# Passages between two graph layers placed three loop steps earlier, with two pairs of their steps put into one step each

## The reference, cut to what matters

```python
# layer 0
A = a * adj, with 1 - a added to the diagonal
y = (A / rowsum(A)) @ x
x1 = layernorm(x + relu(y @ W.T + b))
# layer 1
t = logmap0(x1)                      # a factor for each row: needs the row's norm, a log, some divisions
par = adj   * sigmoid(t @ w_par[:d] [:, None] + t @ w_par[d:] [None, :] + b_par)
chi = adj.T * sigmoid(t @ w_chi[:d] [:, None] + t @ w_chi[d:] [None, :] + b_chi)
out = layernorm(x1 + proj(expmap0(chi @ t + par @ t)))
```

## Time and profile before

| | before |
|---|---|
| median of 3 runs | 2226.71 us (2226.44 to 2228.95) |
| the profiled execution | 2229.62 us, its span 2227.6 us |
| mean granted clock of PE | 0.979 of full speed |
| busy, share of the span | PE 91%, DVE 87%, POOL 60%, ACT 59% |
| from the start to the last panel's evacuation (L938) | 1271.1 us |
| late phase | 956.5 us |

### The profile page before, as it was taken

One profiled execution on the slowest core, in us unless ns is written; L12 is line 12 of the kernel. 1 busy time (PEld: TensorE's weight loads), 2 busy tenths in 40 slices (PEclk: granted clock), 3 DMA queues, 4 the chain that ended last, 5 costly groups with the idle time before them and its releaser, 6 DMA issues. The chain is left out here.

```text
span 2227.6 us, 18363 instructions
## 1 busy us (share of the span) xinstructions
PE 2022.5 (91%) x5088; PEld 898.5 (40%) x5088; DVE 1941.7 (87%) x1856; ACT 1323.2 (59%) x1508; POOL 1336.0 (60%) x639
## 2 busy tenths in 40 slices
PE   7999999999989998999999967998888888889886
PEld 3444444444434433444444433333333334334432
DVE  5657788988989898899898989998998989989897
ACT  0001324354364454444434578998888989999996
POOL 0000304534455445643543577999998999999996
PEclk9999999999999999999999988999999999999998
DMA  9978988989989988988978998999999999999993
GB/s 339 354 280 282 391 298 348 377 345 377 379 318 407 375 345 351 375 331 342 392 322 345 394 412 329 417 421 421 421 415 400 421 414 409 421 422 394 401 386 158
DMA packets 128356, 820.36 MB, mean 368 GB/s; under 512 B 14832, under 2 KB 27376, under 8 KB 31232
## 3 DMA queue, kind: packets, MB, share of 16 engines
q1 hardware_dynamic: 113392, 799.06, 89.0%
q10 hardware_dynamic: 14864, 20.13, 2.7%
HBM read 814.88 MB, written 4.26 MB: 368 GB/s over the span
## 5 line engine op out<-in xcount | busy, mean ns | idle before, releaser
L547 POOL TENSOR_TENSOR chi<-chi,ring 128x1024 f32<-128x1024 f32 x326 | 830.1, 2561 | 662.6 <-ACT chi L753 609.9
L1237 PE MATMUL ps<-keys,xtA 128*128 128x512 f32 x2048 | 981.4, 611 | 146.0 <-DVE keys L1039 109.9
L1165 PE MATMUL ps<-ring,xA 128*128 128x512 f32 x2048 | 922.6, 600 | 40.4 <-DMA ring<-in_g_blk 21.5
L770 ACT ACTIVATE ps<-scores,prcr 128x1024 f32<-128x1024 f32 x492 | 544.0, 1106 | 406.1 <-DVE keys L1039 388.7
L1237 PEld LDWEIGHTS ps<-keys,xtA 128*128 128x128 f32 x2048 | 378.0, 193 | 690.3 <-issue 650.8
L933 DVE TENSOR_TENSOR dsum<-dsum,ring 128x2048 f32<-128x2048 f32 x240 | 595.0, 2479 | 33.7 <-DMA ring<-in_g_blk 27.6
L1165 PEld LDWEIGHTS ps<-ring,xA 128*128 128x128 f32 x2048 | 388.6, 192 | 534.5 <-issue 496.0
L1039 DVE TENSOR_TENSOR keys<-ps,chi 128x1024 f32<-128x1024 f32 x426 | 521.5, 1224 | 83.8 <-issue 33.1
L753 ACT ACTIVATE chi<-scores,prcr 128x1024 f32<-128x1024 f32 x426 | 483.7, 1135 | 14.9 <-DMA scores<-plcl_d 8.7
L1030 DVE TENSOR_TENSOR ps<-ps,ring 128x1024 f32<-128x1024 f32 x348 | 425.4, 1222 | 61.0 <-ACT ps L770 58.8
L547 POOL TENSOR_TENSOR chi<-chi,xA 128x1024 f32<-128x1024 f32 x79 | 185.9, 2370 | 18.6 <-ACT chi L753 18.6
(11 more groups left out here) (121 smaller groups left out, 808.5 us busy)
## 6 DMA issues: line engine op xcount, KB each, us to landing
ring<-in_g_blk SPq DMA_DIRECT2D x443, 1024.0 KB, 8.7
ring<-in_a_cols SPq DMA_DIRECT2D x190, 1024.0 KB, 9.8
xA<-in_a_cols SPq DMA_DIRECT2D x51, 1024.0 KB, 11.2
xA<-in_g_blk SPq DMA_DIRECT2D x44, 1024.0 KB, 9.3
scores<-in_a_cols SPq DMA_DIRECT2D x15, 1024.0 KB, 11.0
scores<-in_g_blk SPq DMA_DIRECT2D x15, 1024.0 KB, 9.6
scores<-plcl_d ACTq DMA_DIRECT2D x22, 512.0 KB, 10.2
xA<-in_x_g ACTq DMA_DIRECT2D x64, 64.0 KB, 9.9
```

Source lines behind the costliest of these rows:

```text
L547: pool.tensor_tensor(out=chi(n), in0=chi(n), in1=half(t, n), op=ALU.mult).then_inc(m2_ready, 1)
L770: act.activation(dst, scores[:, row, 0, :], ACT.Sigmoid, bias=prcr[:, 2 * jt:2 * jt + 1]).then_inc(p_ready, 1)
L1165: ins = pe.matmul(Y[:, h * BANK:(h + 1) * BANK], xA[:, tile * D:(tile + 1) * D], t[:, tt * BP + h * BANK:tt * BP + (h + 1) * BANK], start= ...
L1237: ins = pe.matmul(outp[:, h * BANK:(h + 1) * BANK], xtA[:, jt * D:(jt + 1) * D], keys(n)[:, h * BANK:(h + 1) * BANK], start=begins, stop=i ...
```

## The change

The table of ticks gets other numbers. `statistics` moves to the tick of `residual` (both 6), `norms` to the tick of `squares` (both 10), and what stands between and behind moves up by one, two or three pairs: `deviation` 8 -> 7, `normalise` 10 -> 9, `logarithm` 14 -> 12, `tangent` 16 -> 14, the turn 18 -> 16, the row scores 22 -> 20, their copy 23 -> 21, `load_rows` 25 -> 22. Units become due three pairs earlier (`T_UNITS` 22 -> 19, `T_OWN` 27 -> 24). In the tables of the late phase the two merged steps lose their own entries and run with their partners; all other entries keep their distance from the start of the phase. No instruction of a step is changed.

```diff
 (T_EVAC, T_FOLD, T_DEG, T_INV, T_LIN, T_RES, T_STATS, T_STD, T_RSTD, T_X1, T_SQ, T_NRM, T_LOGA, T_LN, T_FAC, T_XT,
- T_TURN, T_XTT, T_PRP, T_PRCR, T_ROWS, T_COPY, T_LOADL) = (0, 0, 1, 2, 4, 6, 7, 8, 9, 10, 11, 12, 13, 14, 15, 16,
-                                                           18, 18, 19, 20, 22, 23, 25)
+ T_TURN, T_XTT, T_PRP, T_PRCR, T_ROWS, T_COPY, T_LOADL) = (0, 0, 1, 2, 4, 6, 6, 7, 8, 9, 10, 10, 11, 12, 13, 14,
+                                                           16, 16, 17, 18, 20, 21, 22)
-T_UNITS = 22
-T_OWN = 27
+T_UNITS = 19
+T_OWN = 24
```

More of the change, by code:

```diff
@@ L44 @@
 (T_EVAC, T_FOLD, T_DEG, T_INV, T_LIN, T_RES, T_STATS, T_STD, T_RSTD, T_X1, T_SQ, T_NRM, T_LOGA, T_LN, T_FAC, T_XT,
- T_TURN, T_XTT, T_PRP, T_PRCR, T_ROWS, T_COPY, T_LOADL) = (0, 0, 1, 2, 4, 6, 7, 8, 9, 10, 11, 12, 13, 14, 15, 16,
-                                                           18, 18, 19, 20, 22, 23, 25)
+ T_TURN, T_XTT, T_PRP, T_PRCR, T_ROWS, T_COPY, T_LOADL) = (0, 0, 1, 2, 4, 6, 6, 7, 8, 9, 10, 10, 11, 12, 13, 14,
+                                                           16, 16, 17, 18, 20, 21, 22)
 T_LOADX, T_SCALEX = 25, 29
-T_UNITS = 22
-T_OWN = 27
+T_UNITS = 19
+T_OWN = 24
 LATE_PE = {2: T_DEG, 6: T_LIN, 27: T_TURN, 31: T_PRP, 34: T_ROWS}
-LATE_ACT = {14: T_STD, 17: T_X1, 19: T_SQ, 21: T_NRM, 24: T_LN, 27: T_XT, 32: T_XTT, 39: T_COPY}
-LATE_DVE = {5: T_INV, 10: T_RES, 11: T_STATS, 14: T_RSTD, 21: T_LOGA, 24: T_FAC, 34: T_PRCR}
+LATE_ACT = {14: T_STD, 17: T_X1, 19: T_SQ, 24: T_LN, 27: T_XT, 32: T_XTT, 39: T_COPY}
+LATE_DVE = {5: T_INV, 10: T_RES, 14: T_RSTD, 21: T_LOGA, 24: T_FAC, 34: T_PRCR}
 def early_groups():
```

## The result

The change makes the kernel a little slower. The median is 2233.59 us (12 runs, 2231.62 to 2237.92) against 2226.57 of the kernel before (12 runs, 2219.59 to 2230.17); the ratio is 1.0032, with a 95% interval of 1.0023 to 1.0041, so +7.0 us. The profiled execution took 2234.92 us, its span is 2233.1 us, the mean granted clock 0.981 (before 0.979).

A forecast was written before the change was run, and what follows sets the result against it. PE was taken to bound panels 1 to 7, with ring and copy stalls in 4 to 7, and transfers the late phase. 5.1 - 7.4 - 6 - 6 + 1 + 1 = -12.3 from 2226.7 gave 2214.4 us, range 2204 to 2229.

The forecast's parts named there:

- Three units into panel 1, +5.1: Panel 1: three units moved in cost PE 3 x 1.71 us, as PE has no time to spare there.
- Three units out of the late phase, -7.4 and +1: Late phase: three units fewer save 3 x 2.47 us (-7.0 to -9.5); one unit's addition returning to DVE costs 1.
- the late merges: Late phase: statistics and norms run with their partners, the same work a unit earlier, 0 us, bounds +3 and -3.
- as the sum of what the two cost apart: Squares with norms on ACT: 5.1 us at once costs no more than 2.3 and 2.8 apart; at worst 2.3 more.
- The copies at pair 5 have no step of ACT ahead of them: Group-end copies: 1.5 us waits at pair 8 in panels 4, 6, 7 go; panel 4 counts nothing, the ring's stall growing equally.
- Panel 5, -6: Panel 5: the copy leaves its place behind `tangent`, so its 6.51 us wait and clock loss go; between 0 and -7.1.
- only the trade of units: Rival, chance 0.21: stalls in panels 5 to 7 stay, set by DVE's chain; about 2226 us, 2222.5 to 2231.
- Panels 6 and 7, -3 each: Passages of panels 6 and 7: of 7.6 us lost, -3 each, as units without a gap end at pair 10, not 13.
- about 11 us and no more: Passages of panels 4 to 7: the ring covers a DVE lag behind PE of about 11 us, then PE waits.
- slower: Rival, chance 0.12: merged steps overrun the ring, 5 x 5.3 us, about 2246; sign: PE idle over 13 us in panel 4.

The follow-up runs named there:

- the norms apart: The changed kernel with norms two units behind squares in the late phase alone, statistics staying with residual: 2227.79 us, ratio 1.0006.
- the one panel of the kernel before that got such an end: Panel 5 of the kernel before with units due five pairs later (ticks 27 and 32), which put a copy at pair 29 there alone: 2234.43 us, 1.0042.
- the best kernel: The changed kernel with copy behind sigmoids, evacuation ahead of the last pair's first product, late merges undone, norms one pair behind squares in panels: 2206.13 us, 0.9912.
- the norms apart in the panels: The changed kernel with norms one pair behind squares in the panels (tick 11), late phase keeping the merge: 2228.93 us, ratio 1.0015.
- the kernel with units and ends back: The changed kernel with units due at ticks 22 and 27 as before, group ends again at pairs 0, 8, 16 and 24: 2237.17 us, 1.0053.

## Why the prediction was wrong

The forecast was 2214.4 us with faster at 0.72; 2233.59 lies above its range. By its steps:

- **Three units into panel 1, +5.1: right.** Panel 1 measured +5.2.
- **Three units out of the late phase, -7.4 and +1: right in sum, by luck, wrong in its parts.** The late phase fell by 6.9. But with the norms apart it falls from 956.5 to 943.6, by 12.9, and the merge takes 6 of that back. The term for the units was too small, and the late merges, which I had at 0 with bounds of +3 and -3, cost twice the bound. The phase's start is faster: 19 units in the first 60 us, 18 before. PE's waits for copies in the first 135.9 us are 9.1 us before and 3.4 after, since a group's end stands elsewhere; that this is what speeds up the start was not tried by itself.
- **Merges "as the sum of what the two cost apart": the wrong end of a bound that had been named.** The prediction said that a half that ACT hid twice might be hidden once, up to 2.3 us in each of four panels and in the late phase, and took 0. Squares with norms cost 4.7 us in the panels and 5.8 late. The mechanism was the one named; late it went beyond the bound, and a meeting of DVE with POOL behind the pause may be a part of that (last section). The price of the switch of the function table is not what was missed: the merged step's two took 1345.01 to 1347.83, 2.8 us for both with the norms between them, as in the earlier trace rows. The Trainium skill ("ScalarE: Activation LUTs", What ACT_TABLE_LOAD costs) has some 2.66 us for each; these rows do not agree.
- **"The copies at pair 5 have no step of ACT ahead of them", and nothing for pair 29: the step that failed most.** I asked what holds the copy, and not whom the copy holds. ACT takes things in order, and `take_out` stands ahead of the pair's sigmoids; a copy that waits for PE makes DVE and POOL wait for ACT. At pair 29 DVE has two pairs left to catch up in before the evacuation, which stands behind `dsum` and a unit's product in its order. That copies would stand at pair 29 was known, and nothing was priced for it. The six panel ends come 17.4 us late in all, 3.0 before; the one panel of the kernel before that got such an end is late by 3.1; exchanging copy and sigmoids gives 13.2 us back.
- **Panel 5, -6: came to nothing.** The wait behind `tangent` went from 6.51 to 1.76 us, as foreseen, and the ring took its place. The waits of PE in panel 5, before and after:

```profile
PE ps L1237 <- ACT taken L786: 7.8, 2, 6.5
PE ps L1165 <- DMA ring<-in_g_blk: 4.1, 2, 2.4
```

```profile
PE ps L1165 <- DMA ring<-in_g_blk: 6.9, 5, 3.2
PE ps L1237 <- ACT taken L786: 1.8, 1, 1.8
...
```

With the rows left out (3.3 us for `xtA`, keys and `yb`) these are 11.9 and 12.0 us; by the windows PE is idle 11.9 and 14.3, some 2.2 of the latter with no wait recorded. This is the rival "only the trade of units", whose reason was that a copy that no longer waits lets PE run into the next limit. In the best kernel the panel still has 187.80 - 176.40 = 11.4 us of idle PE, with one copy of 8.5. DVE is busy 177.77 of the 187.80 us there; that this is the reason is argued and not shown.
- **Panels 6 and 7, -3 each: the mechanism stood, covered by the rest.** The lag of DVE at pair 7 was to be 9.1 us; it is 996.12 + 2.28 - 989.21 = 9.2. It did not stop at 11: at pair 11 it is 1020.88 + 2.28 - 1010.20 = 13.0 (rows with the norms apart in the panels), and PE did not wait for the ring, so "about 11 us and no more" did not hold there. (Panel 6 carries units up to pair 10 and from 19 on, not beside every pair as the section on the change says at one place.) The waits of the passage are 1.96 and 1.79 us in panel 6, less than the 4.6 that the term left standing. But panel 6 begins with PE's wait for the late end of panel 5, and behind it 4 matmuls take 3.75 us, about twice the 1.96 of four at full clock, which is the lower level:

```profile
946.66 3.75 PE L1165 MATMUL ps<-ring,xA 128*128 128x512 f32 x4 [3.73 <-DVE yb L938]
```

With copy, evacuation and norms mended the two panels take 163.9 us each, inside the 163 to 166 of the prediction.
- **The rival "slower"** foresaw lumps that overrun the ring and the point where PE is idle 13 us in panel 4. Idle is 185.60 - 177.44 = 8.2 there and PE's wait for the ring fell in panels 2 to 7. The result was on its side, in part by its price for squares and norms, and for the rest by a mechanism that no rival had.

What stays open: the kernel with units and ends back is 10.9 us over before. The two prices measured in the kernel after, 4.7 and 5.8, come to 10.5 and would explain it; but the same merges cost 5.2 in the kernel before. Where the other 5 us lie was not separated: its trace accounts for 5.4 us (2.8 in panels 2 to 7, 3.4 in the late phase, less 0.8 in panel 0), since the profiled execution of the kernel before lies above its median and this one's below. Nor does the sum of single steps close on the 27.5 us between after and the best kernel: 13.2, 6.0, 5.8 and 4.7 are 29.7, and copy and evacuation share the same delay.

## What to carry to other kernels

When a step moves, ask of each thing that moves with it not only what it waits for, but what stands behind it on its in-order engine and which deadline comes next there: a copy that waits for PE, placed ahead of the sigmoids, cost 2.2 us in the kernel where none stood shortly ahead of a panel's end, and 13.2 in the one where six did. Put an engine's waiting steps behind the steps that feed others. One pause twice as long on the engine that feeds the rest cost more here than two pauses (4.7 and 5.8 us), so give a merged step the upper price unless a row shows that length being hidden; and when stalls are removed one by one, count what PE waits for in all, since the next limit stands ready.

## What the runs showed of the hardware

A small operation of DVE took thirteen times its time beside POOL. In the late phase of after, behind the pause of ACT, POOL runs three products without a gap:

```profile
1353.74 6.96 POOL L547 TENSOR_TENSOR chi<-chi,ring 128x1024 f32<-128x1024 f32 x3
...
1356.16 2.27 DVE L978 TENSOR_SCALAR small<-small 128x8 f32<-128x8 f32 x1
...
1358.47 2.26 DVE L979 TENSOR_SCALAR small<-small 128x8 f32<-128x8 f32 x1
```

With the norms apart the same operation comes while POOL stands:

```profile
1351.33 0.17 DVE L979 TENSOR_SCALAR small<-small 128x8 f32<-128x8 f32 x1
...
1352.20 7.00 POOL L548 TENSOR_TENSOR chi<-chi,ring 128x1024 f32<-128x1024 f32 x3 [2.39 <-ACT chi L754]
```

(its lines are numbered one higher). An operation of 0.17 us takes 2.27 and ends at 1358.43, where the second of POOL's three should end (two thirds of 6.96 us behind 1353.74 are 1358.38); the next takes 2.26 more, and when POOL is through at 1360.70 they are short again (0.20 us at 1360.77, 0.17 at 1361.00). `dsum` shows it with a long operation: alone it takes 2.28 us (1099.50 in before); at 1110.93 in after, where POOL's products end at 1112.01, it takes 3.23. The Trainium skill ("SBUF — State Buffer", SBUF: two separate sides) says that DVE and POOL share a pair of ports as an exclusive lock: of an operation of POOL and one of DVE that needs the pair (one in a 2-port mode, or one with two inputs in SBUF), whichever starts first holds it for the whole instruction and the other is blocked. These rows agree, the ends at 1358.43 and 1358.38 above all.

The six operations of `log_map_argument` take 6.3 us in after, from 1355.10 to 1361.37, and 1.2 with the norms apart, from 1351.13 to 1352.35. POOL then runs three products without a gap there too, but the six are through before them. So what the late merge costs may be in part the length of ACT's pause and in part that these steps of DVE fall beside POOL's work; how the 5.8 us divide was not measured.
